# Weight preparation and first maxima inside the projections, rows turned by DMA, a fourth bank for W1's product

## What is computed

```python
def attn(h, Wqvk, Wo):
    qvk = (h @ Wqvk).reshape(b, s, 3, H, HD)
    q, v, k = (qvk[:, :, 0], qvk[:, :, 1], qvk[:, :, 2])
    scores = (q k^T + causal mask) / sqrt(512)
    return (softmax(scores) @ v).reshape(b, s, d) @ Wo
def ffn(x, W1, b1, theta, wr, wi, W2, b2):
    hidden = x @ W1 + b1
    q = hidden + (cos(theta) * wr + sin(theta) * wi) * wi * sin(theta + hidden * 0.1) * 0.1
    return relu(q) @ W2 + b2
x = x + layernorm(attn(layernorm(x), Wqvk, Wo))
x = x + layernorm(ffn(layernorm(x), W1, b1, theta, wr, wi, W2, b2))
```

## Time and profile before

| | |
|---|---|
| time of 3 runs | median 3528.13 us (3526.57 to 3529.32) |
| time of the profiled execution | 3526.83 us |
| its span, first to last instruction | 3524.9 us |
| PE busy | 3214.6 us, 91% |
| DVE / ACT / POOL busy | 2246.1 / 2065.8 / 1322.6 us |
| projections | 40.65 to 567 us on PE |
| attention's main work | 593 to 2072 us |
| last phase | 2072.4 to 3524.9 us |

### The profile page before, as it was taken

One profiled execution on the slowest core, in us unless ns is written; L12 is line 12 of the kernel. 1 busy time (PEld: TensorE's weight loads), 2 busy tenths in 40 slices (PEclk: granted clock), 3 DMA queues, 4 the chain that ended last, 5 costly groups with the idle time before them and its releaser, 6 DMA issues. The chain is left out here.

```text
span 3524.9 us, 78007 instructions
## 1 busy us (share of the span) xinstructions
PE 3214.6 (91%) x29997; PEld 1863.1 (53%) x29997; DVE 2246.1 (64%) x4230; ACT 2065.8 (59%) x2452; POOL 1322.6 (38%) x702
## 2 busy tenths in 40 slices
PE   5999996899898989899899838999999999999998
PEld 2444442676666666667676613444444444444443
DVE  5444444777777777777777446666666666666665
ACT  2222221888888887979797914554554545455453
POOL 0000001798989797979798910000000000000000
PEclk9999997899999999999999968999999999999999
DMA  3344334122222222222223040000000000000000
GB/s 129 111 143 133 114 126 115 40 66 86 64 79 70 77 69 81 61 86 61 87 61 88 28 158 1 24 25 25 24 24 24 24 24 24 24 24 24 24 25 24
DMA packets 183098, 219.97 MB, mean 62 GB/s; under 512 B 15184, under 2 KB 129936, under 8 KB 182288
## 3 DMA queue, kind: packets, MB, share of 16 engines
q1 hardware_dynamic: 182800, 215.83, 19.7%
...
## 5 line engine op out<-in xcount | busy, mean ns | idle before, releaser
L953 POOL TENSOR_TENSOR a_prob_lo<-a_prob,a_prob_hi 128x2048 f16<-128x2048 f32 (+2 forms) x448 | 1192.1, 2691 | 217.3 <-ACT a_prob_hi L851 215.6
L873 DVE TENSOR_REDUCE a_mx<-a_pw 128x1 f32<-128x512 f32 (+3 forms) x1216 | 753.8, 657 | 156.5 <-PE a_pw L728 116.3
L841 ACT ACTIVATE a_prob<-a_pst,a_lift,a_exp_scale 128x1024 f32<-128x1024 f32 (+1 forms) x640 | 709.5, 1123 | 234.5 <-PE a_pst L782 126.4
L1387 PE MATMUL f_py<-f_w,f_act 128*128 128x512 f16 x3072 | 706.9, 380 | 22.8 <-DVE f_work L1153 12.8
L1377 PE MATMUL f_ph<-f_xT,f_w 128*128 128x512 f16 x3072 | 705.8, 380 | 0.0
L851 ACT ACTIVATE a_prob_hi<-a_prob 128x2048 f16<-128x2048 f32 (+2 forms) x448 | 583.0, 1302 | 0.0
L1325 ACT ACTIVATE f_hidden_work<-f_ph,f_turn,f_fold 128x512 f32<-128x512 f32 x256 | 199.2, 778 | 596.3 <-PE f_ph L1377 595.6
L1108 POOL TENSOR_TENSOR f_ve<-f_mv,f_eps 128x4 f32<-128x4 f32 x32 | 9.0, 282 | 1385.4 <-DVE f_mv L1134 1385.4
L723 PE MATMUL a_pw<-a_kp,a_qp 96*128 96x512 f16 (+3 forms) x1536 | 467.1, 340 | 47.7 <-DVE a_mx L873 35.2
L804 PE MATMUL a_acc<-a_vt,a_prob_hi 128*128 128x33 f16 x9216 | 466.4, 178 | 47.4 <-POOL a_prob_lo L953 26.9
L804 PEld LDWEIGHTS a_acc<-a_vt,a_prob_hi 128*128 128x128 f16 x9216 | 432.6, 97 | 128.8 <-DVE a_o L892 27.9
...
## 6 DMA issues: line engine op xcount, KB each, us to landing
qk_parts<-q_stage SPq DMA_DIRECT2D x128, 256.0 KB, 2.2
...
a_vt<-v_parts SPq DMA_DIRECT2D x32, 528.0 KB, 4.3
q_x<-in_L_attn_h_dram SPq DMA_DIRECT2D x16, 1024.0 KB, 7.8
a_xr<-in_L_attn_h_dram SPq DMA_DIRECT2D x64, 256.0 KB, 3.0
x<-a_y SPq DMA_DIRECT2D x64, 256.0 KB, 2.1
```

What stands on the lines that cost most here:

```text
L841: act.activation(prob[:, k % PR, :, off:QC], pst[:, k % 2, :, off:QC], ACT.Exp, scale=exp_scale[:, :], bias=lift[:, :]).then_inc(exp_done, 1)
L873: dve.tensor_reduce(out, src, AX_X, ALU.max).then_inc(released, 1)
L953: pool.tensor_tensor(prob_lo[:, first % HR:first % HR + steps, :, off:QC], prob[:, first % PR:first % PR + steps, :, off:QC], prob_hi[:, f ...
L1387: last = pe.matmul(py[:, t, :], act_r[:, f % AR, b, t * P:(t + 1) * P], w2s[:, a, f, :], start=(f == 0 and j == 0), stop=(f == NF - 1 and ...
```

## The change

- The preparation of Wo, W1, W2 and of the four vectors moves into chunks 6 to 14 of the projections, in 9 pieces (`load_piece`, `largest`, `piece_high`, `piece_low`, `store_piece`). The halves of W1 and W2 are written to DRAM (`w_parts`), and the last phase loads them from there ready-made. `wblock` and the last phase's preparation are gone.
- The constants and the loads of attention's first two units (`first_units`) are issued at the head of chunk 9, and the 39 items of `AHEAD` are interleaved with the 12 products of chunk 15: 3, 3, 3, 3, 3, 3, 3, 3, 4, 4, 4, 3.
- No transposes on PE in the projections and in the last phase: ACT and DVE split the normed rows in halves first (`upper`, `lower`, the first chunk's low halves on POOL in the projections), and a DMA with transpose (`turn`) brings each block of 128 rows, 128x1024 float16 or 256 KB, into `xT`.
- The first six products of the projections run with k outside, so that each quarter of the weights is used as soon as it is split (`first_outputs`).
- `ph` has four banks (HB = 4) in place of three and the bank of the transposes.

```diff
+                def turn(n, e, t):
+                    sp.wait_ge(x_lo, TPC * n + t + 1)
+                    sp.sem_inc(turning, 1)
+                    sp.dma_start(xT[:, e, :, :, t * P:(t + 1) * P], xh[:, t, :, :].rearrange("p a d -> p (a d)"),
+                                 transpose=True).then_inc(xT_loaded[e], 16)
+                def turns(n, e, m):
+                    if m == QK - 3:
+                        turn(n + 1, 1 - e, 0)
+                    elif m == QK - 2:
+                        turn(n + 1, 1 - e, 1)
+                    elif m == QK - 1:
+                        turn(n + 1, 1 - e, 2)
+                        turn(n + 1, 1 - e, 3)
...
+                def load_piece(job):
+                    if SLOTS <= job < PIECES_W + SLOTS:
+                        sp.wait_ge(piece_max, job - SLOTS + 1)
+                    elif job >= PIECES_W + SLOTS:
+                        sp.wait_ge(piece_lo, job - SLOTS - PIECES_W + 1)
...
+                def store_piece(job):
+                    piece = job - PIECES_W
+                    if piece > 0:
+                        sp.wait_ge(piece_lo, piece + 1)
+                        sp.dma_start(weights.parts[piece - 1], halves[:, piece % 2]
+                                     ).then_inc(piece_stored[piece % 2], 16)
+                def pieces(n, m):
+                    job = job_at(n, m - 2)
+                    if job is not None:
+                        if job >= PIECES_W:
+                            store_piece(job)
+                        if job + SLOTS < 2 * PIECES_W:
+                            load_piece(job + SLOTS)
+                def store_peeled(i, e):
+                    n = 2 * i + e
+                    for m in range(QK):
+                        sp.wait_ge(out_lo, MM * n + m + 1 + MM)
+                        sp.dma_start(qk_parts[i, m].rearrange("l p t -> p l t")[:, :, e * CH:(e + 1) * CH],
...
+                        pieces(n, m)
+                        if n < NCH - 1:
+                            turns(n, e, m)
...
+                def first_units():
+                    for s in stored:
+                        sp.wait_ge(s, 16 * (QK // STAGE) * CPB + START)
+                    for u in range(2):
+                        for c in range(CPB):
+                            load_qk(sp, units, qk_parts, 0, u, c, True)
+                            load_qk(sp, units, qk_parts, 0, u, c, False)
+                    sp.wait_ge(v_stored, 16 * CPB + START)
+                    for u in range(2):
+                        load_v(sp, units, v_parts, 0, u)
+                    for t in range(2):
+                        load_x(sp, units, x.rearrange("b (t p) d -> b t p d", p=P), 0, t)
...
+                for t in range(TPC):
+                    turn(0, 0, t)
...
+                        if 2 * i + e == LOAD_CHUNK:
+                            first_units()
+                        store_peeled(i, e)
+                sp.wait_ge(units.released, len(AHEAD))
+                store_max(sp, units, 0)
...
+                def lower(n, e, t):
+                    dve.wait_ge(x_hi, TPC * n + t + 1)
+                    dve.tensor_tensor(xh[:, t, 1, :], xin[:, e, t, :], xh[:, t, 0, :], ALU.subtract).then_inc(x_lo, 1)
...
+                        if isinstance(n, int):
+                            first_maxima(first_items(n, m)[:2])
...
+                            first_maxima(first_items(n, m)[2:])
...
+                def piece_low(job):
+                    piece = job - PIECES_W
+                    which = LIMIT[piece]
+                    dve.wait_ge(piece_hi, piece + 1)
+                    dve.scalar_tensor_tensor(split_piece(piece, 1), slot(job), scale[:, which:which + 1],
+                                             split_piece(piece, 0), ALU.mult, ALU.subtract).then_inc(piece_lo, 1)
...
+                def upper(i, n, e, t):
+                    if t == 0:
+                        act.wait_ge(normed, n + 1)
+                        act.wait_ge(xT_loaded[1 - e], 16 * TPC * i + 16 * TPC)
+                    act.activation(xh[:, t, 0, :], xin[:, e, t, :], ACT.Copy).then_inc(x_hi, 1)
...
+                def piece_high(job):
+                    piece = job - PIECES_W
+                    which = LIMIT[piece]
+                    act.wait_ge(piece_loaded[job % SLOTS], 16 * (job // SLOTS + 1))
+                    if piece == 0:
+                        act.wait_ge(centred, 4)
+                    if piece > 2:
+                        act.wait_ge(piece_stored[piece % 2], 16 * ((piece - 1) // 2))
+                    act.activation(split_piece(piece, 0), slot(job), ACT.Identity, scale=scale[:, which:which + 1]
+                                   ).then_inc(piece_hi, 1)
...
-                def transposes(n, e, k, first=False):
...
-                        pe.wait_ge(normed, n + 1)
-                    for t in range(TPC):
-                        last = pe.transpose(pt[:, k % 2, t * P:(t + 1) * P], xin[:, e, t, k * P:(k + 1) * P], ident[:, :])
-                    last.then_inc(tr_done, 1)
...
+                        pe.wait_ge(xT_loaded[e], 16 * TPC * i + 16 * TPC)
...
+                def first_outputs():
+                    pe.wait_ge(xT_loaded[0], 16 * TPC)
+                    for k in range(KT):
+                        pe.wait_ge(w_lo, k + 1)
+                        for m in range(BANKS):
+                            for a, b in PASSES:
+                                last = product(0, m, k, a, b, start=(k == 0 and (a, b) == PASSES[0]),
+                                               stop=(k == KT - 1 and (a, b) == PASSES[-1]), skip_group_check=True)
+                            if k == KT - 1:
+                                last.then_inc(mm_done, 1)
...
+                def first_item(at, what, piece):
...
+                    if at >= 2:
+                        pe.wait_ge(units.released, at - 1)
+                    if what == "piece":
+                        last = score_piece(pe, units, pt[:, at % 2], 0, piece)
+                    else:
+                        pe.wait_ge(units.max_ready, 1)
+                        last = turn_maxima(pe, units, pt[:, at % 2])
+                    last.then_inc(units.work_done, 1)
...
+                    for m in range(MM):
+                        if not (first and m < BANKS):
+                            output(i, n, e, m)
+                        if isinstance(n, int):
+                            for at, (what, piece) in first_items(n, m):
+                                first_item(at, what, piece)
...
-        with nc.Block() as wblock:
...
-            @wblock.sync
-            def _(sp):
-                for k in range(KT):
-                    sp.dma_start(raw[:, k, :], w_o[k * P:(k + 1) * P, :]).then_inc(w_loaded[k], 16)
-                first_units(sp)
...
-    HB = 3
+    HB = 4
...
-    TR_AT = {11: 0, 12: 1, 13: 2, 14: 3}
+    HALVES_AT = {10: 0, 11: 1, 12: 2, 13: 3}
...
+                def turns(n, e):
+                    for t in range(TPC):
+                        sp.wait_ge(x_lo, TPC * n + t + 1)
+                        sp.sem_inc(turning, 1)
+                        sp.dma_start(xT[:, e, :, :, t * P:(t + 1) * P], xh[:, t, :, :].rearrange("p a d -> p (a d)"),
+                                     transpose=True).then_inc(xT_loaded[e], 16)
...
+                def load_w1(g):
+                    cols = slice(g * QF * P, (g + 1) * QF * P)
+                    for k in range(KT):
+                        sp.dma_start(w1s[:, :, k, cols], weights.parts[k][:, :, cols]).then_inc(w1_loaded[g], 16)
...
+                def load_w2(g):
+                    sp.dma_start(w2s[:, :, g * QF:(g + 1) * QF, :],
+                                 weights.parts[KT + g].rearrange("p a (k d) -> p a k d", k=QF)
+                                 ).then_inc(w2_loaded[g], 16)
...
-                for n, v in enumerate((b1, phases, w_real, w_imag)):
-                    sp.dma_start(vec_rows[n * NF:(n + 1) * NF, :], v.rearrange("(f p) -> f p", p=P)
-                                 ).then_inc(vec_loaded, 16)
-                for n in range(KT):
-                    sp.dma_start(raw[:, n, :], w1[n * P:(n + 1) * P, :]).then_inc(w_loaded[n], 16)
                 load(0, 0)
-                for g in range(NF // 4):
-                    sp.dma_start(raw[:, KT + g, :].rearrange("p (k d) -> p k d", k=4),
-                                 w2.rearrange("(g k p) d -> g p k d", k=4, p=P)[g]).then_inc(w_loaded[KT + g], 16)
+                load_w1(0)
+                load_w2(0)
+                load_w1(1)
+                turns(0, 0)
+                load_w2(1)
+                for g in range(2, 4):
+                    load_w1(g)
+                    load_w2(g)
                 sp.dma_start(b2s[:, :], b2_rows).then_inc(b2_loaded, 16)
                 load(1, 1)
+                turns(1, 1)
...
+                        turns(2 * i + e + 2, e)
...
+                for t in range(TPC):
```

(6 more changed lines are left out.)

1205 lines of the change are left out of this document (622 added, 583 removed).

## The result

| | before | after |
|---|---|---|
| median of 4 runs | 3528.70 us (3526.57 to 3529.32) | 3446.95 us (3442.96 to 3449.3) |
| ratio, 95% interval | | 0.9768 [0.9751, 0.9785] |
| profiled execution, its span | 3526.83, 3524.9 us | 3445.31, 3443.5 us |

The account below looks back on a forecast made before the run. PE bounds the projections and last phase, with stretches between and at the start where it waits for preparation. Terms -14.4 - 26.2 - 34 - 24 - 26.2 + 12 = -112.8 take 3526.8 to 3414 us; range 3380 to 3485.

Parts of the forecast that it names:

- Rival 1: Whole kernel: the terms act as summed, 3414 us, with bounds 3383 to 3451; chance 0.60.
- Rivals 2 and 3: Turns too slow: 3.3 to 5.2 us of queue each (3474 at 4.3), chance 0.18; beyond 5.2, slower (3789 at 7.8), 0.16.
- Start of the projections: PE's first product starts at 26.2 us in place of 40.65; gain 14.4 us (10 to 16).
- Transposes off PE: Projections and last phase: four groups of 0.44 us leave PE in each of 15 chunks; gain 26.2 us in each stretch.
- Moved work: Weight pieces and units' loads in the projections: queue delays cost 9 us at chunk 9, 3 in chunks 10 to 14; +12.
- Rival 4: Prepared work collides in the queue, chunks 9 to 14 losing 6 to 10 us more each; about 3460 us, chance 0.06.
- a budget of their own: Projections: the last block's turn has 5.6 us for landing, four turns up to 3.3 us of queue each; no stall.
- the chain that the prediction named: Chunk 9: stores wait behind the units' loads, ACT for a slot, DVE for ACT; 9 us lost (0 to 20).
- Hand-over: Last chunk's first product to attention's first scores falls from 90.0 to 56 us; gain 34 (24 to 40).
- Start of the last phase: First `output` starts 47 us after the phase's start in place of 71.3, set by b2's load at 42; gain 24 (15 to 39).
- Last phase: Turns have up to 6.05 us of queue each, so PE does not idle on them before a chunk's `output(0)`.
- Fourth bank: Last phase: PE never waits for `ph`, so a fourth bank gains 0.

Follow-up runs that it names:

- copy_turns_ahead: Changed kernel with plain copies for transposing DMAs, a turn issued ahead of a weight piece's store and load in the written-out chunks; 3437.21 us, ratio 0.9745.
- copy_pieces_early: Changed kernel with plain copies for transposing DMAs, the first three 1 MB weight pieces loaded before the projections' loop; 3437.21 us, ratio 0.9750.
- copy_act_queue: copy_units_spread with weight pieces' loads and stores and the first units' loads issued by ACT on its own queue; 3432.71 us, ratio 0.9737.
- pe_turns: Changed kernel with both sets of turns back on PE and three banks for W1's product; 3469.80 us, ratio 0.9833.
- copy_units_spread: Changed kernel with plain copies for transposing DMAs, the first two units' loads issued one pair after each of chunks 7 to 12; 3432.90 us, ratio 0.9740.
- copy_joined: Changed kernel with plain copies for transposing DMAs plus the edits of copy_b2_first, copy_units_spread, copy_turns_ahead and copy_shift together; 3409.22 us, ratio 0.9663.
- copy_shift: Changed kernel with plain copies for transposing DMAs, 16 idle products on PE ahead of attention's first scores; 3432.89 us, ratio 0.9731.
- copy_b2_first: Changed kernel with plain copies for transposing DMAs, b2's load moved from behind all last-phase weights to behind the first rows; 3429.62 us, ratio 0.9727.

## Why the prediction was right, and where it was off

**The rivals.** Rival 1 held. Rivals 2 and 3 needed a turn of over 3.3 us of queue; its landing is 3.0 us in chunks 1 to 5 (4.1 in 245:535), and by the shares it takes 1.65. So no wait of the first seven chunks ends on a turn, as rival 1 has it; those behind are the next terms' matter. The bounds of rival 1 were added up wrongly by 3 us: to one side they give -147, not -144. The judgement by the nearest rows (2.2 and 4.3 us for 256 KB and for 1024 packets) was right. The Trainium skill's figure of 1309 ns for a 128x128 block (VectorE: DVE Perf Modes, "The three transpose paths"), an estimate of 10.5 us for a turn, is not what this trace shows: eight blocks land within 3.0 us. Its 261 GB/s (DMA: Bandwidth & Descriptors, "Latency and other measured facts"), an estimate of 1.0 us, is nearer, and too low a time: 256 KB in 1.65 us are 159 GB/s.

**Start of the projections**, forecast 14.4: measured 14.3, 26.36 against 26.2, on the quarter's low half as put.

**Transposes off PE**, 26.2 twice: 24.3 and 27.4 by the table. The 24.3 are an effect of the mean: an undisturbed chunk went from 32.83 to 31.08 us, the 1.75 that the term has (4 x 0.44), and 26.6 in all.

**Moved work**, forecast +12, measured +35.2 (37.5 by undisturbed chunks): the term that was mis-sized, and the step that failed. The prediction charged the loads of the units at 9 and the pieces at 3, these in chunks 10 to 14 only; the nine loads of the first pass over the weights, for the maxima, which begin ahead of chunk 6's stores, have no term. Rival 4 holds the pieces against "a chunk where DMA is idle 63%", the share of the trace before, and the turns have a budget of their own, chunk by chunk; the two were never added to one sum. The sum was to be had: 12.2 us of DMA in a chunk before, 4 turns at the 2 to 3 us that the prediction itself allowed, and 3 to 4 MB of pieces at 222 to 424 GB/s come to over 27 of 31 us; the trace shows 85%. The theory that took its place first, that transfers stand behind others in one queue, explains little: copy_turns_ahead and copy_pieces_early changed the order and took 3.0 and 1.6 us off PE's waits, and in copy_act_queue the stores landed as late from a queue without the weights. What moved the time more was the load on the DMA engines: pe_turns takes the turns off it and loses 22.6 where the changed kernel loses 35.2, copy_units_spread lowers its highest peak for 5 to 7, and only then is the order worth 4.3 (copy_joined). The rest, 19 us even in copy_joined (546.0 - 15 x 31.35 - 56.75), stays open: no kernel ran without the weights' traffic or with more slots in `q_stage`.

The wait in chunk 9 came by the chain that the prediction named (stores late, slot, DVE, PE): "9 us (0 to 20)". It is 7.2 within the chunk and 4.75 before the next. What was left out is chunks 7, 8 and 12, with 8.5, 2.1 and 3.6. Rival 4, 6 to 10 us more in each of chunks 9 to 14 (+46), is the same in kind; the 23 us missed are half of it, and part of them fall in chunks 7 and 8, outside its chunks.

**Hand-over**, 34: measured 33.2, 56.75 us against 56, 50.9 of it to the turn of the maxima (48 forecast) and 5.9 behind it (8).

**Attention**, not spoken of in the prediction, so forecast 0: +11.5. Five turns of the loop took 2.4 us more each. copy_shift shows that most of it comes with the instructions that stand ahead of the loop, and not from the work that was moved: 16 products put ahead took 9.4 us off the five turns and 7.9 off B. Some 4 us over the kernel before are left (B 1451.3 without the products, for 1447.3), within the scatter of 6. What it is about the place, the trace does not tell by itself: in the changed kernel the second wait comes behind the first four products of the loop, as if the code ended there for a while. The Trainium skill (Runtime: NRT & Kernel Launch, "Instruction fetch mechanics") says that instructions are fetched sequentially in blocks of 256, and that a taken branch to code outside of the blocks at hand stalls until the target's block is there. A loop head close to the end of such a block would give two waits, and 32 instructions more (a product and its weight load, 16 times) would move it into the next. This agrees with both traces; that it is the cause was not shown, since no row tells where a block ends.

**Start of the last phase**, 24: measured 28.9, `output(0)` 42.4 us after the first load in place of 47. The mechanism was as put, DVE waiting for b2 while `hidden(0)` starts at 21.3 (21 forecast), and copy_b2_first confirms it; mis-sized was b2's landing, 37.0 in place of 42. The sum took 222 GB/s for W1's runs of 1 KB; the whole stretch moved 278 GB/s on average. **Last phase**: no wait for a turn after the first chunk, as put. **Fourth bank**: 0, confirmed.
